# First stage of a decoder kernel: exponential's table, keys before values, and another order on VectorE

## What is computed

```python
x = x + attn_ref(layernorm(x), ...)         # first stage: the change is here
x = x + xattn_ref(layernorm(x), ctx, ...)   # cross attention
x = x + ffn_ref(layernorm(x), ...)          # experts

# attn_ref(src):
q, k, v = split(layer_norm(src) @ qkv_w + qkv_b)      # 16 heads of 8
qf, kf = elu(q) + 1, elu(k) + 1
kv, z = sum_n kf*v, sum_n kf                          # per head
y = (qf @ kv) / max(qf . z, 1e-6)
x = src + y @ out_w + out_b
return x + gelu(layer_norm(x) @ w1 + b1) @ w2 + b2
```

## Time and profile before

| | |
|---|---|
| median of 3 runs | 885.07 us |
| profiled execution, whole | 887.35 us |
| its span, first to last instruction | 885.5 us |
| mean granted TensorE clock | 0.963 of 2.4 GHz |
| PE busy | 796.6 us (90%) |
| VectorE busy | 634.9 us (72%) |
| ScalarE busy | 462.7 us (52%) |
| GpSimd busy | 539.9 us (61%) |

### The profile page before, as it was taken

How to read it: one execution, slowest core, us unless ns; L and a number is a source line. 1 busy time by engine, 2 the same in 40 slices (tenths; PEclk the granted TensorE clock), 3 DMA queues, 4 the chain that set the end, 5 groups by cost and what they waited for, 6 DMA issues and landing times.

```text
span 885.5 us, 26095 instructions
## 1 busy us (share of the span) xinstructions
PE 796.6 (90%) x9363; PEld 601.8 (68%) x9363; DVE 634.9 (72%) x2079; ACT 462.7 (52%) x771; POOL 539.9 (61%) x747
## 2 busy tenths in 40 slices
PE   3799999999999999999999999985299999989993
PEld 2577777777666777777777777774177667766772
DVE  6788888888856788888888888866155555455552
ACT  1366666666646777777777777663132222322330
POOL 3357575656553326667667766656566666477765
PEclk9799999999999999999999999997599999999997
DMA  7349990000000001111100101110434544466650
GB/s 235 99 132 390 390 370 2 0 0 0 2 1 3 14 15 63 64 69 45 41 31 31 34 30 39 38 52 30 146 122 127 155 132 135 119 198 190 208 173 5
DMA packets 51249, 86.99 MB, mean 98 GB/s; under 512 B 12953, under 2 KB 29145, under 8 KB 51144
## 3 DMA queue, kind: packets, MB, share of 16 engines
q1 hardware_dynamic: 38784, 72.15, 24.5%
q0 software_dynamic: 11264, 12.70, 4.4%
q10 hardware_dynamic: 1096, 0.73, 0.3%
HBM read 42.04 MB, written 58.41 MB: 113 GB/s over the span
## 4 chain that ended last, share of the span: by engine, by line
PE 56%; POOL 13%; issue 11%; DVE 10%; ACT 6%; DMA 1%; DVEq 1%; POOLq 1%; ACTq 0%; SPq 0%
PE psum L2090 15%; PE psum L2102 8%; PE psum L638 6%; POOL dispatched L875 5%; PE psum L617 4%; PE psum L1583 3%; POOL rs L865 3%; PE psum L2084 2%; PE psum L1544 2%; ACT z L1384 2%; PE psum L1563 2%; ACT L534 2%; PE psum L1530 2%; PE psum L649 2%; DVE top_score L1017 2%
## 5 line engine op out<-in xcount | busy, mean ns | idle before, releaser
L1987 POOL DMA_INDIRECT out<-yo,token x160 | 158.2, 989 | 71.0 <-issue 40.3
L875 POOL DMA_INDIRECT dispatched<-z,idx x128 | 129.7, 1013 | 72.0 <-issue 48.1
L1403 ACT ACTIVATE PT<-psum,key_bias 77x1024 f32<-77x1024 f32 x128 | 135.0, 1102 | 52.0 <-PE psum L1566 51.7
L2069 ACT ACTIVATE act_g<-psum 128x512 f32<-128x512 f32 x80 | 47.6, 597 | 160.2 <-PE psum L2090 141.1
L1563 PE MATMUL psum<-qT,Kb 32*77 32x128 f32 x2048 | 121.5, 278 | 0.0
L1017 DVE TENSOR_REDUCE top_score<-psum 128x8 f32<-128x616 f32 x128 | 101.7, 795 | 18.8 <-PE psum L1544 16.4
L1544 PE MATMUL psum<-Kb,qT 32*128 32x308 f32 x512 | 99.5, 461 | 1.7 <-DVE qT L1041 0.4
L2025 DVE SCALAR_TENSOR_TENSOR yo<-psum,xin,base 128x128 f32<-128x128 f32 x156 | 43.9, 344 | 79.3 <-PE psum L2102 79.1
L1563 PEld LDWEIGHTS psum<-qT,Kb 32*77 32x77 f32 x2048 | 91.4, 143 | 0.7 <-DVE X L461 0.5
L1566 PE MATMUL psum<-MT,minus_sel 32*77 32x128 bf16 x1024 | 90.3, 214 | 0.0
L2102 PE MATMUL psum<-down,h 128*128 128x128 f32 x640 | 79.8, 279 | 3.3 <-DVE h L2040 3.3
(11 more groups left out here) (217 smaller groups left out, 1733.1 us busy)
## 6 DMA issues: line engine op xcount, KB each, us to landing
dispatched<-zeros SPq DMA_DIRECT2D x40, 522.0 KB, 7.2
xin<-dispatched SPq DMA_DIRECT2D x39, 522.0 KB, 4.8
out<-zeros SPq DMA_DIRECT2D x20, 256.0 KB, 3.0
first<-out SPq DMA_DIRECT2D x20, 256.0 KB, 4.3
X<-in_x SPq DMA_DIRECT2D x16, 256.0 KB, 2.7
out<-X SPq DMA_DIRECT2D x16, 256.0 KB
out<-yo,token POOLq DMA_INDIRECT x160, 3.1
ctx<-in_ctxT SPq DMA_DIRECT2D x4, 616.0 KB, 6.0
```

The lines of the kernel that those rows point to most:

```text
L875: pool.indirect_dma_start(xg[k], bass.IndirectOffsetOnAxis(ap=idx[n % Z4][:, t, k:k + 1], axis=0), z4[n % Z4][:, t, :], None, bounds_check ...
L1403: nc.scalar.activation(PT[j % 2][:, half * HB * 2 * P:(half + 1) * HB * 2 * P], T[:, 2 * half:2 * half + 2, :].rearrange("p a c -> p (a c) ...
L1987: pool.indirect_dma_start(rows_out if slot else out, bass.IndirectOffsetOnAxis(ap=token[i][:, t:t + 1], axis=0), yo[i][:, t, :], None, bou ...
```

## The change

Five edits in the first stage:

1. ScalarE runs a one-column Exp (`bring_exponential`) behind the four Gelu of every turn that has a group g-1 and a group g+2. The same function takes the place of the start's one-column Exp.
2. `project_kv` makes all keys first (bank 0, semaphore `k_ps`) and then all values (bank 1, `v_ps`): 128 columns a matmul in place of 256, each tile's weights loaded for both.
3. VectorE adds the keys' bias right behind `finish`, and the values' bias after the statistics of group g+2; `k_features` follows it. The aggregation of those statistics goes behind `k_features` (before the values' bias for g below 0).
4. `mask_kv` goes in front of `ln2_stats`.
5. The open mean goes from the hook "moments" (in front of the key bias) to the hook "end", the turn's last work.

```diff
-        kvp = psum[:, 0:2, :].rearrange("p a (b c) -> p (a b) c", b=2)
+        k_bank, v_bank = (banks[i].rearrange("p (t c) -> p t c", t=G4) for i in range(2))
...
                 if group(g - 2):
                     finish(g - 2)
                 between(g, "finish")
+                if group(g + 1):
+                    add_k_bias(g + 1)
                 if group(g + 2):
+                    ln0_stats(g + 2)
+                if isinstance(g, int) and g < 0 and group(g + 2):
                     ln0_moments(g + 2)
                 if isinstance(g, int) and g == -1:
                     clear_values(1)
+                if group(g + 1):
+                    add_v_bias(g + 1)
+                    k_features(g + 1)
+                if group(g + 2) and (not isinstance(g, int) or g >= 0):
+                    ln0_moments(g + 2)
                 between(g, "moments")
                 if group(g + 1):
-                    add_kv_bias(g + 1)
-                    k_features(g + 1)
                     q_features(g + 1)
                 if group(g):
                     add_attention(g)
-                    ln2_stats(g)
                 if group(g + 1):
                     mask_kv(g + 1)
                 if group(g):
+                    ln2_stats(g)
                     ln2_moments(g)
                 between(g, "end")
...
+            def bring_exponential():
+                nc.scalar.activation(table[:], minus_one[:], ACT.Exp)
...
                 if group(g - 1):
                     gelus(g - 1)
+                    if group(g + 2):
+                        bring_exponential()
...
-                for t in range(G4):
-                    last = nc.tensor.matmul(kvp[:, t, :], ln1T[:, t * P:(t + 1) * P], qkv_w[:, P:3 * P], start=True, stop=True)
-                last.then_inc(s["kv_ps"], 1)
+                for bank, at, done in ((k_bank, P, "k_ps"), (v_bank, 2 * P, "v_ps")):
+                    for t in range(G4):
+                        last = nc.tensor.matmul(bank[:, t, :], ln1T[:, t * P:(t + 1) * P], qkv_w[:, at:at + P], start=True, stop=True)
+                    last.then_inc(s[done], 1)
...
-                if place == "moments" and group(g - 1):
+                if place == "end" and group(g - 1):
...
                     mean_of_open(g - 1)
```

More of the change, by code:

```diff
@@ L177, in linear_attention_and_ffn @@
         minus_one = sb("minus_one_col", [P, 1])
+        table = sb("table", [P, 1])
         v1 = sb("v1", [P, G4, SIDES, SP + 1])
@@ L185, in linear_attention_and_ffn @@
                  "ln0_stats ln0_moments ln0_var ln0_rstd z1_ready n0_ready n0b_ready z1T_ps ln1T_ready "
-                 "q_ps kv_ps q1_ready eq_ready qf_ready k1_ready v_ready ek_ready kf_ready "
+                 "q_ps k_ps v_ps q1_ready eq_ready qf_ready k1_ready v_ready ek_ready kf_ready "
                  "KV_ps KV_ready y_ps den_ready rden_ready y_ready yT_ps yT_ready attn_ps x1_ready x1b_ready xs_ready "
@@ L338, in xrow, with ln0_stats @@
                 return X[:, bass.ds(G4 * g + t, 1), :].rearrange("p a c -> p (a c)")
-            def ln0_moments(g):
+            def ln0_stats(g):
                 dve.wait_ge(s["x_loaded"], 16 * g + 16)
@@ L347, in ln0_moments @@
                 last.then_inc(s["ln0_stats"], 1)
+            def ln0_moments(g):
                 dve.wait_ge(s["ln0_stats"], g + 1)
@@ L379, in q_features, with add_k_bias @@
                 nc.vector.scalar_tensor_tensor(qf[:], eq[:], 1.0, q1[:], ALU.min, ALU.max).then_inc(s["qf_ready"], 1)
-            def add_kv_bias(g):
-                dve.wait_ge(s["kv_ps"], g + 1)
+            def add_k_bias(g):
+                dve.wait_ge(s["k_ps"], g + 1)
                 if some(g):
@@ L385, in add_kv_bias, with add_v_bias @@
                     dve.wait_ge(s["kf_ready"], g)
-                nc.vector.tensor_tensor(k1[:], kvp[:, :, 0:P], over(kb_row[:], 1, G4), ALU.add).then_inc(s["k1_ready"], 1)
+                nc.vector.tensor_tensor(k1[:], k_bank, over(kb_row[:], 1, G4), ALU.add).then_inc(s["k1_ready"], 1)
+            def add_v_bias(g):
+                dve.wait_ge(s["v_ps"], g + 1)
                 if some(g):
                     dve.wait_ge(s["KV_ps"], g)
-                nc.vector.tensor_tensor(v1[:, :, :, 0:SP], kvp[:, :, P:2 * P].rearrange("p t (f c) -> p t f c", f=SIDES),
+                nc.vector.tensor_tensor(v1[:, :, :, 0:SP], v_bank.rearrange("p t (f c) -> p t f c", f=SIDES),
                                         over(vb_row[:].rearrange("p (f c) -> p f c", f=SIDES), 1, G4), ALU.add).then_inc(s["v_ready"], 1)
@@ L506, in ln1T_side @@
                     act.wait_ge(s["q_ps"], g)
-                    act.wait_ge(s["kv_ps"], g)
+                    act.wait_ge(s["v_ps"], g)
                 nc.scalar.activation(ln1T[:], tp, ACT.Identity, scale=g1, bias=be1).then_inc(s["ln1T_ready"], 1)
@@ L562, in scalar @@
             act.wait_ge(s["neghalf_ready"], 1)
-            nc.scalar.activation(ek[:, 0, 0:1], minus_one[:], ACT.Exp)
+            bring_exponential()
             act.wait_ge(s["first_loaded"], n_first)
```

## The result

The changed kernel takes 895.38 us (median of 6 runs, 893.87 to 899.28) where the kernel before, run beside it, takes 885.01 (6 runs, 882.83 to 888.23): a ratio of 1.0111, 95% interval 1.0086 to 1.0135. It is slower. The forecast was 882.0. The profiled execution of the changed kernel took 894.52 us, its span is 892.7, and its mean granted clock 0.961.

A forecast was written before the change was run, and what follows sets the result against it. The loop was taken as closed by VectorE's order and two ScalarE steps, though PE looks full. Loop -6.6, start +2.5, tail +0.8 and +0.2 gave -3.1 us: 885.07 to 882.0, range 879.0 to 888.0 (forecast's own 878.8 to 885.6).

The forecast's parts named there:

- VectorE's loop: First-stage loop: VectorE's steps of 8.80 us plus PE's transposes-to-keys stretch were summed to 13.91 us, fitting PE's 14.09 by 0.18.
- second rival: PE's transposes L579 wait for z1 (L363) behind the open mean; loop wins less, up to 888.6 us; chance 0.15.
- The branch: The loop's branch on VectorE, counted at 0.34 us a turn in the sum for VectorE's loop.
- The start: First turns of the first stage: key bias ahead of statistics and memset loses 2.5 us, bounds 1.5 and 4.2.
- The term of turn -1: Turn -1: VectorE waits for keys before statistics and memset, so context comes at 21.8 instead of 19.65, 2.15 us late.
- 0.3 in turn 0: Turn 0: the statistics, which filled a wait for PE, come behind the keys, for some 0.3 us more.
- third rival: A colder start: turn 0 or 1 runs once more at PE's lower clock, another 1.73 us, 883.7; chance 0.12.
- The wait for Gelu: Second `ffn_up` half on PE waits for Gelu, 7.1 us over the stage, 0.52 a loop turn; predicted gone.
- the loop is PE's: PE's own order was to set the loop turn: floor 14.09 us against 14.64, winning 0.55 a turn.
- The tail behind attend(14): Turn 13: mean and swapped `ln2` statistics delay z1's transposes; 0.8 us lost, bounds 0 and 1.3.
- the 0.2 of turn 15: Turn 15: the mean pushes the first cross keys by 1.33 us, past PE's first use; 0.2 lost, bounds 0 and 0.3.
- first rival: Three table loads a turn: the Exp load before `eq` stays in the loop, 1.7 us won, 3.5 lost, 886.9; chance 0.15.

## Why the prediction was wrong, and where it was right

**VectorE's loop: the step that failed.** The forecast counted the mean at its old durations (0.53 for its first step) and argued against its second rival that "each duration above is already one taken beside a running GpSimd". That it ran beside GpSimd was true; beside which of GpSimd's instructions, and for how long, was not asked: 0.19 us beside `xs`, which had already brought it from 0.45 to 0.53. The move put `kept`, which reads two tiles from SBUF, beside a 1.27 us addition that also reads two, and it took 1.26. The text had followed the moved aggregation to the roots on GpSimd, but not on to `n0b` behind the root: it moved from right behind x1 to just ahead of the mean. The Trainium skill (SBUF — State Buffer, Who interferes with whom) states that a VectorE instruction with two SBUF inputs contends with a GpSimd instruction that reads SBUF. The traces agree for GpSimd's two additions: `kept` took 0.45 with nothing beside it, 0.48 behind a 0.21 us addition, 1.26 beside the long one; beside GpSimd's root they show no such delay (last section). In the kernel with the aggregation early `kept` and `n0b` overlapped only for the last 0.46, and `kept` took 0.80. Where the collision is taken away, the forecast's sum for the loop, with the branch put right, holds to 0.02.

**The branch** was kept at 0.34. It is 0.62 in the steady turns with the mean last, in all five kernels that have it there, and 0.48 with the aggregation last and a wait in front of it: 0.28 that the sum lacked. That it belongs to the loop and not to z1 is seen in the written-out turns, where z1 follows without such idle time (226.91 in the earlier trace rows).

**The second rival** named the right place (t1 waiting for z1) and half of the right trigger, "beside GpSimd's bias and roots" (it was the bias), at a chance of 0.15. Its price was wrong: it stopped at 14.64, as if VectorE's loop could not become longer than the old turn. It came to 14.90.

**The start** was costed at +2.5 and measured +5.42. The term of turn -1 was right: 2.15 forecast, 2.74 less the 0.5 of the later landing measured. What failed is that the rest was taken to lose little, 0.3 in turn 0 and nothing behind it: turn 1 took 2.27 more, of it 1.27 in key and value matmuls at the low clock (3.16 against 1.89) and a part in waits for z1 and z2. That is the third rival (a colder start, priced at 1.73) on top of the forecast, not in its place: the granted clock was 0.50 from 39 to 49 us, with PE busy 7.6 of these 10, and the key and value matmuls began at 46.40 in it; in the kernel before they began at 41.84, as it came back from 0.50 to 1.00. The rival took the 3.62 us of turn -1 for the lower clock as well; the profile has 1.00 there, in both kernels, so the length of that row stays unexplained. In the four other kernels with this start attend(2) is 3.2 to 4.4 us later than before, so one to two of the 5.42 us belong to this execution. By the experiment with the old order the start also hid a gain of about 3 us.

**What was right.** The wait for Gelu is gone. With the mean moved back the loop is PE's: 14.05 measured, 14.09 forecast; with the mean last and no collision it is VectorE's, at 14.12. The key bias waits for PE and starts 1.10 behind the first key matmul, where 1.1 was forecast. The tail behind attend(14) cost 1.22, 0.8 forecast with bounds of 0 and 1.3; the 0.2 of turn 15 is lost in the differences of the later stages. The first rival, three table loads a turn, fell: L518 and L551 load 14 times each, and none stands before `eq`. The rival's price for a load before `eq` came close in the experiment without the early Exp: 14.5 worked out, 14.60 measured. The Trainium skill (ScalarE activation tables, Table sets in the compiler and the runtime) says that loads are placed per block, from which the prediction took it that the loop body would reload; this loop, which has Exp's table at both ends, does not.

## What to carry to other kernels

When an instruction moves in one engine's order, follow every engine that waits for it to the end of its queue, and list what then runs at the same moment as what: a duration read at one place holds at another only beside the same neighbours, overlapping them for as long. An order that is good in the steady loop can be bad in the first turns, where the awaited data are late and there is work to fill the wait; write the two orders separately and read each from its own rows. Two limits at nearly the same time must be moved together: here either alone gave 0.04 us a turn or less, and both 0.59.

## What the runs showed of the hardware

`kept` was not slowed in proportion: it was held until GpSimd's instruction ended, and ended 0.33 to 0.34 us behind it, in the changed kernel, in the one with the aggregation early and, behind `xs`, in the kernel before. It takes what is left of the other instruction and a third of a microsecond, in place of 0.45, so the price depends on the instant of the start. It goes the other way too: in the kernel with the aggregation early, GpSimd's small step L281 started at 123.07 beside the key features (123.08 to 123.76) and took 0.74 in place of 0.19, to 0.05 behind their end. Not every overlap costs: with the mean moved back, `qf`, which reads two tiles, ran from 107.97 inside GpSimd's root (107.59 to 109.26) in its usual 0.69. The runs do not show why the root is different. The loop's branch on VectorE costs between 0.34 and 0.62 us a turn, by what stands last in the turn; the runs show that, not why.
